# Layer-norm rows from VectorE to ScalarE, attention's value products two steps at a time, and ScalarE's pair copies between its two exponentials

## What is computed

```
def _layernorm(x, axis=-1, eps=1e-05):
    m = jnp.mean(x, axis=axis, keepdims=True)
    v = jnp.var(x, axis=axis, keepdims=True)
    return (x - m) / jnp.sqrt(v + eps)
...
    h = _layernorm(x, axis=-1) * (1 + ca) + sa
    x = x + ga * _L0_attn_ref(h, ...)      # q, k l2-normed; softmax(q k^T / 8) v; Wo; bo
    h = _layernorm(x, axis=-1) * (1 + cb) + sb
    x = x + gb * _L0_ffn_ref(h, ...)       # router, top 2 of 8 experts, capacity, shared expert
```

## Time and profile before

| | |
|---|---|
| three runs | 1409.37, 1414.08, 1416.97 us (median 1414.08) |
| the profiled execution: its own time, its span | 1406.78 us, 1405.0 us |
| mean granted TensorE clock | 0.959 |
| busy: PE, PEld | 1262.1 us (90%), 828.6 us (59%) |
| busy: DVE, ACT, POOL | 1107.3 us (79%), 952.9 us (68%), 858.0 us (61%) |
| idle of TensorE before line L585 until VectorE's L810 | 33.2 us, 14 times |

### The profile page before, as it was taken

The page is one execution under the profiler, slowest core; times in us unless marked ns, Lnnn a source line. Parts: engine busy times, 40 slices in busy tenths (PEclk is TensorE's granted clock), DMA queues, the critical chain, the costliest instruction groups (busy, mean ns, idle before and its releaser), DMA issues. The chain is left out here.

```text
span 1405.0 us, 31811 instructions
## 1 busy us (share of the span) xinstructions
PE 1262.1 (90%) x9674; PEld 828.6 (59%) x9674; DVE 1107.3 (79%) x1995; ACT 952.9 (68%) x2014; POOL 858.0 (61%) x1659
## 2 busy tenths in 40 slices
PE   4899999989999999999899999999994477899997
PEld 4555565656555565556566555666552355677775
DVE  3778878878878887788788788877873996788887
ACT  3677677767666776677677766777762565777776
POOL 2577666766666776666667667676754664444443
PEclk8899999999999999999999999999998699999999
DMA  5000000000000000000000000000002000535341
GB/s 131 2 2 1 2 1 2 2 4 2 1 4 2 2 2 4 2 2 2 4 1 2 3 2 2 2 1 2 2 1 75 1 0 9 131 86 104 89 89 38
DMA packets 53202, 28.60 MB, mean 20 GB/s; under 512 B 8720, under 2 KB 51224, under 8 KB 53016
## 3 DMA queue, kind: packets, MB, share of 16 engines
q1 hardware_dynamic: 51832, 25.99, 7.7%
q10 hardware_dynamic: 1184, 0.40, 0.1%
HBM read 24.16 MB, written 2.23 MB: 19 GB/s over the span
## 5 line engine op out<-in xcount | busy, mean ns | idle before, releaser
L697 ACT ACTIVATE probs<-bank,neg_max 128x512 f32<-128x512 f32 x512 | 347.5, 684 | 280.3 <-DVE neg_max L815 259.5
L815 DVE TENSOR_REDUCE neg_max<-bank 128x1 f32<-128x512 f32 x512 | 329.3, 685 | 165.4 <-PE bank L516 162.0
L556 PE MATMUL bank<-probsT,qkv 128*64 128x512 f32 x1024 | 280.7, 628 | 0.9 <-DVE oT L832 0.9
L516 PE MATMUL bank<-operands 64*128 64x512 f32 x1536 | 255.9, 439 | 0.9 <-DVE operands L810 0.5
L993 POOL TENSOR_TENSOR inv_wide<-inv_sum,consts 128x512 f32<-128x512 f32 x64 | 66.5, 1039 | 237.7 <-DVE inv_sum L826 237.7
L532 PEld LDWEIGHTS T<-ident,probs 64*128 64x128 f32 x4096 | 173.6, 142 | 40.3 <-issue 10.2
L532 PE MATMUL T<-ident,probs 64*128 64x64 f32 x4096 | 173.6, 226 | 1.5 <-issue 0.7
L486 PEld LDWEIGHTS bank<-operands,hT_h 128*128 128x128 f32 x254 | 48.2, 190 | 213.0 <-issue 209.4
L516 PEld LDWEIGHTS bank<-operands 64*128 64x128 f32 x1536 | 128.4, 190 | 63.5 <-issue 44.2
L1627 POOL TENSOR_TENSOR hid_l<-gated,hid_h 128x512 fp32r<-128x512 f32 x64 | 89.4, 1397 | 123.3 <-ACT hid_h L1544 123.3
L977 POOL TENSOR_TENSOR sq<-qkv 128x256 f32<-128x256 f32 x252 | 150.9, 615 | 11.9 <-ACT qkv L676 9.7
(11 more groups left out here) (235 smaller groups left out, 2399.7 us busy)
## 6 DMA issues: line engine op xcount, KB each, us to landing
probsT<-gate_scratch SPq DMA_DIRECT2D x64, 256.0 KB, 4.9
out<-x_all SPq DMA_DIRECT2D x8, 256.0 KB, 2.3
probsT<-in_L_ffn_fc_w SPq DMA_DIRECT2D x1, 1024.0 KB, 9.4
raw<-in_L_attn_Wq SPq DMA_DIRECT2D x1, 512.0 KB, 4.4
raw<-in_L_attn_Wk SPq DMA_DIRECT2D x1, 512.0 KB, 7.3
raw<-in_L_attn_Wv SPq DMA_DIRECT2D x1, 512.0 KB, 8.6
raw_o<-in_L_attn_Wo SPq DMA_DIRECT2D x1, 512.0 KB, 8.7
probsT<-in_L_ffn_sh_w SPq DMA_DIRECT2D x2, 256.0 KB, 2.7
```

The lines of the kernel that those rows point to most:

```text
L516: last = nc.tensor.matmul(s_bank(hp, 2 * pair + head)[:], own[rows, q, toks], own[rows, k], start=((q, k) == (QH, KH)), stop=(q == QL))
L556: last = nc.tensor.matmul(O_BANK[rows, :], qkv[:, hp % 4, j, cols], probsT[:, hp % 2, head, j], start=(j == 0), stop=(j == NT - 1), skip_g ...
L697: nc.scalar.activation(probs[:, i % 4], s_bank(hp, i)[:], ACT.Exp, bias=neg_max[:, i:i + 1], accum_out=row_sum[:, hp % 2, i:i + 1]).then_i ...
L815: nc.vector.reduce_max(neg_max[:, i:i + 1], s_bank(hp, i)[:], AX.X, negate=True).then_inc(max_done, 1)
```

## The change

Three edits. First, the rows of the layer norm: VectorE additionally writes the negative mean (4 numbers a row of partitions), GpSimd multiplies it by the inverse deviation (`ln_shift`) after its Newton iteration, and ScalarE computes x * rstd + shift in four instructions of 128x128 in place of VectorE's four. ScalarE does this in the same pair, after its copy of k and ahead of its exponentials; in the opening stage it does so after its sixth weight copy, and after the last slot ahead of `modulate2`. Second, TensorE does steps 2 and 3 of the value products together in pair 0, and steps 0 and 1 together in pair 2; pairs 1 and 3 have none. Third, ScalarE's copy of T2 in pairs 1 and 3 stands between the two exponentials of the pair instead of behind both.

```
             def aggregate(dve, count):
...
                 nc.vector.tensor_scalar(var_eps[:], mean_var[:, :, 1], LN_EPS, None, ALU.add).then_inc(ve_done, 1)
+                nc.vector.tensor_scalar(neg_mean[:], mean_var[:, :, 0], -1.0, None, ALU.mult).then_inc(nm_done, 1)
...
-            def ln_rows(dve, b, count):
-                dve.wait_ge(ln_step, NEWTON_OPS * (count + 1))
-                after(dve, hlnT_ready, count)
+                pool.wait_ge(nm_done, count + 1)
+                pool.wait_ge(ln_step, NEWTON_OPS * (count + 1))
+                nc.gpsimd.tensor_tensor(ln_shift[:], neg_mean[:], rstd[:], ALU.mult).then_inc(shift_done, 1)
+
+            def ln_rows(act, b, count):
+                act.wait_ge(shift_done, count + 1)
+                after(act, hlnT_ready, count)
                 for t in range(NT):
-                    last = nc.vector.tensor_scalar(h_ln[:, t], tile_of(b, t), mean_var[:, t, 0:1], rstd[:, t:t + 1],
-                                                   ALU.subtract, ALU.mult)
+                    last = nc.scalar.activation(h_ln[:, t], tile_of(b, t), ACT.Identity, scale=rstd[:, t:t + 1],
+                                                bias=ln_shift[:, t:t + 1])
                 last.then_inc(hln_done, 1)
...
-                            if pair < 2 and earlier >= 2:
-                                weigh_values(u - 2, hp - 2, pair + 2)
-                            if pair >= 2 and earlier >= 1:
-                                weigh_values(u - 1, hp - 1, pair - 2)
+                            if pair == 0 and earlier >= 2:
+                                weigh_values(u - 2, hp - 2, 2)
+                                weigh_values(u - 2, hp - 2, 3)
+                            if pair == 2 and earlier >= 1:
+                                weigh_values(u - 1, hp - 1, 0)
+                                weigh_values(u - 1, hp - 1, 1)
...
+                            if main and pair == 3 and norm_of(b, hp):
+                                ln_rows(act, *norm_of(b, hp))
                             if main:
                                 exponentials(u, hp, 2 * pair)
-                                exponentials(u, hp, 2 * pair + 1)
                             if pair == 1 and earlier >= 1:
                                 copy_transposed(u - 1, hp - 1, 3)
                             if pair == 3 and main:
                                 copy_transposed(u, hp, 1)
+                            if main:
+                                exponentials(u, hp, 2 * pair + 1)
...
-                            if rows and pair == 3:
-                                ln_rows(dve, *rows)
```

More of the change, by code:

```diff
@@ L155, in adaln_attention_moe @@
             rstd_t = sb("rstd_t", [P, NT])
+            neg_mean = sb("neg_mean", [P, NT])
+            ln_shift = sb("ln_shift", [P, NT])
             st1_done = sem("st1_done")
@@ L161, in adaln_attention_moe @@
             hln_done = sem("hln_done")
+            nm_done = sem("nm_done")
+            shift_done = sem("shift_done")
             hlnT_ready = sem("hlnT_ready")
@@ L297, in _ @@
                                                  ACT.Copy).then_inc(s_wh, 1)
+                            if j == 5:
+                                act.wait_ge(x0_in, 16)
+                                ln_rows(act, 0, 0)
                     @block.vector
@@ L317, in _ @@
                                                     ALU.subtract).then_inc(s_wl, 1)
-                            if j == 5:
-                                ln_rows(dve, 0, 0)
                         dve.wait_ge(s_small, 9 * 16)
@@ L461, in adaln_attention_moe, with norm_of @@
             t_pair = T2[:].rearrange("p a (k q) -> p a k q", q=DH)
+            def norm_of(b, hp):
+                if hp == YT_HP and not is_const(b, 0):
+                    return b - 1, h2_nth(b - 1)
+                if hp == H1T_HP - 1 and not is_const(b, LAST):
+                    return b + 1, h1_nth(b + 1)
+                return None
             with nc.Block() as block:
@@ L662, in _ @@
                     slot(B, 0, main=False)
-                    for j in (2, 3):
-                        weigh_values(HP * B - 1, HP - 1, j)
+                    weigh_values(HP * B - 1, HP - 1, 2)
+                    weigh_values(HP * B - 1, HP - 1, 3)
                     project_out(LAST, 3, (r_copied, HP * B), (y_more, 3 * LAST + 2))
@@ L781, in _ @@
                         high_h2(q)
+                    act.wait_ge(x1_done, B)
+                    ln_rows(act, LAST, h2_nth(LAST))
                     modulate2(LAST)
@@ L881, in first_part @@
                             take_mod(mod2, (GA, GA_BO, CB, SB), b, mod2_done, (h2_done, b))
-                    def norm_of(b, hp):
-                        if hp == YT_HP and not is_const(b, 0):
-                            return b - 1, h2_nth(b - 1)
-                        if hp == H1T_HP - 1 and not is_const(b, LAST):
-                            return b + 1, h1_nth(b + 1)
-                        return None
                     def norm_first(b, hp, pair):
@@ L965, in _ @@
                     guess_std(dve, nth)
-                    ln_rows(dve, LAST, nth)
                     logits(LAST)
```

## The result

The change makes the kernel **slower: 1450.55 us** median of four runs (1443.88 to 1457.74) against 1415.38 of before beside it (1409.37 to 1416.97). The ratio is 1.0257, 95% interval 1.0195 to 1.0319, so it is slower without doubt, and by 2% or more most likely. The forecast was 1431, with 1408 to 1450: the direction was right, the amount some 20 us short, and the median lies 0.5 us outside the range.

What follows compares the result with a forecast made beforehand. TensorE was taken to bound most slots, with VectorE's `low_k` in pair 3 and GpSimd's chain just behind. The terms summed to +17.5 us, so against 1414.1 us the forecast was 1431, range 1408 to 1450.

Steps and rivals of the forecast that it cites:

- 30 ordinary slots: Slots without norm event or loop end: merged products +0.71 us, wait for ScalarE's copy +0.16, so 30 x 0.87 = +26.1.
- twelve norm events of batches 1 to 6: Layer-norm slots 0 and 3, each with the slot behind: six at -0.6 us, six at -0.5, together -6.6.
- norm event of batch 7: The layer-norm event of batch 7: +0.5 us, with less to win because its clock did not fall.
- five ends of the loop body: At the branch TensorE arrives 1.00 us earlier and pair 3 keeps its gain: -0.12 us each, -0.6 together.
- last two slots, slot 0 of batch 0: The last two slots were put at +1.5 us and slot 0 of batch 0 at -1.4.
- opening and tail: Opening stage loses about 0.4 us, the norm after the last slot gains about 2.4: -2.0 together.
- Rival 2: Pair 3 keeps its shortening: 59 slots 1.0 us shorter, 1372 us; chance 0.10.
- rival 5: No effect of the merge, a second product step costs 1.00 us too: 1449 us; chance 0.04 with the rest.
- The four tiles: ScalarE's layer-norm instructions of an event: 0.8 to 3.2 us, taken as 2, costing nothing because GpSimd is later.
- rival 1: GpSimd does not bind the norm slots; an event gives -2.1 us instead of -0.55: 1413 us; chance 0.15.
- -0.5 us for the two slots together: Slots 3 and 4: transposes of q come 1.4 us earlier, the doubled product in pair 2 adds 0.86.
- rival 3: New stalls of about 2 us at L495 bring 1.2 GHz stretches: +13 to +20 us, 1444 to 1451; chance 0.14.

Runs made afterwards that it cites:

- after_again: The changed kernel once more, unaltered, on the same chip as `after_fill`: 1452.27 us, 1.030 of before.
- sq_back: `after_poolsq` with value products merged only in pair 2; steps 2 and 3 stand apart in pairs 0 and 1: 1411.90 us, 1.001 of before.
- after_poolsq: The changed kernel with GpSimd's squares ahead of its split of the attention output in slots 0 and 3: 1419.36 us, 1.005 of before.
- after_fill: The changed kernel plus seven matmuls with unread results ahead of pair 2's projection in slots 1 and 4, batches 1 to 6: 1436.56 us, 1.019 of before.
- sq_front: `after_poolsq` with value products merged only in pair 0; steps 0 and 1 stand apart in pairs 2 and 3: 1381.07 us, 0.979 of before.
- ln_only: The kernel before with the first edit alone, the layer-norm rows on ScalarE: 1390.69 us, 0.985 of before.

## Why the prediction was wrong, and what in it held

The profiled executions differ by +46.8 us, the sum was +17.5 (and 1414.1 + 17.5 is 1431.6, which I put down as 1431). By its own terms:

| term | forecast | measured |
|---|---|---|
| 30 ordinary slots | +26.1 | +32.2 |
| twelve norm events of batches 1 to 6 | -6.6 | +9.9 |
| norm event of batch 7 | +0.5 | +0.5 |
| five ends of the loop body | -0.6 | +3.0 |
| last two slots, slot 0 of batch 0 | +0.1 | +2.7 |
| opening and tail | -2.0 | -1.4 |

In the profile of `after_again`, 5 us shorter, the ordinary slots measure +28.9, the norm events +6.6 and the loop ends +4.0: these terms move by 1 to 3 us from one execution to the next.

**Right.** The ordinary slot: 23 of the 30 (all but slot 5 of batches 1 to 7) measure +0.82 on average against +0.87, with each step where it was put: second product 0.87, pair 1 at its floor of 2.55, the 0.16 us for ScalarE's copy (0.67 more without the third edit), and pair 3 held at S3 + 3.04. `sq_back` shows that last floor is what costs: the merge in pair 2 takes 41 us, the one in pair 0 ten. Rival 2, by which pair 3 would have kept its shortening, is thus refuted, and so is rival 5. The four tiles take 1.64 us, inside my 0.8 to 3.2 and below the 2 that I took; the page "ScalarE: Activation LUTs" of the Trainium skill (what ACT_TABLE_LOAD costs) had given an estimate of 1.6, and the trace agrees. The stall of the norm slots moved and did not go, with GpSimd as its cause; `ln_poolsq` and `after_poolsq` refute rival 1. The tail gave -2.3 for -2.4.

**Wrong: "-0.5 us for the two slots together".** For the norm events I let the old stall take its half clock with it and took none for the new one, though I named that case as rival 3. Where the new stall is followed by the full clock, the term nearly holds: in batch 4 slots 3 and 4 take 15.40 + 18.02 = 33.42 us against 33.47. What is missing to my -0.5 is GpSimd's chain: inversion to inversion 17.62 us, where I had worked out 17.15, because VectorE begins its sum 0.48 behind the end of the squares (504.11 to 504.59) in the event of slot 3. But in five of six batches slot 4 is 1.5 us longer than that, and in three of six slot 1 is 1.5 longer: 5 x 1.46 + 3 x 1.50 = 11.8 us at half clock behind the new stall, which carries most of the norm events' miss of 16.5. `after_fill` tests it without touching any wait of GpSimd: with the stall filled, half clock is gone from slots 1 and 4 in every batch, and 15.7 us of the 21 by which `after_again` (1452.3) exceeds my 1431 go away.

**Wrong as well: +0.87 for slot 5.** I gave the idle time that the merge puts ahead of `between` no price in clock. In slot 5, where the router's narrow matmuls follow it, five of six batches run 1.55 us longer: 7.8 us of what "ordinary slots" lists, and without it they would stand at +24.4. No rival of mine named this place.

With the first of the two, rival 3 came true: I had priced it at 13 to 20 us more, 1444 to 1451. Its price for one event, 1.0 to 1.5, was right, but only 8 of the 12 looped events paid it, 11.8 us, and 1431 + 12 would be 1443; that the time still lies in its band is in part luck, since slot 5, the loop ends and the last slots, which it doesn't name, made up the rest. Its chance of 0.14 was the mistake. My evidence was the wait of 1.89 us at the branch with the full clock behind it, against 2.49 us with half clock in the earlier trace rows. The new stall is 1.81 us, shorter than the one at the branch, and brings half clock in five of six batches in slot 4: the length of a stall alone doesn't tell, so the earlier trace rows was no evidence for another place in the cycle. With a case on either side the rival deserved about even chances, and the range an upper end beyond 1451. The page "TensorE: Matmul & The Clock Gate" of the Trainium skill (the HAM clock gate) says that activity is what releases the clock from its slow default. The experiments agree in slots 1 and 4, where seven matmuls in place of the wait kept the full clock. That idle time added to every slot would cost clock, as I read the rule, they bear out for slot 5 alone; in slots 2, 3 and 6 the same idle time cost none.

**Wrong, and smaller: the loop ends.** TensorE reaches the branch 1.00 us earlier, as I said, but then idles 2.14 to 2.91 us instead of 1.89, with half clock behind one of them: +3.0 instead of -0.6.

**Size and spread.** The four runs of the changed kernel fall in line with their clock: from 109.6 us at half clock in the whole span (1443.9 us) to 145.6 (1457.7), some 0.38 us for each, as expected of `after_again`, whose runs give 0.46. Before ran in a band of 7.6 us, the changed kernel in one of 13.9.

**Open.** Why the idle time at the branch grew; why VectorE's start behind the squares takes 0.48 us in one of the two norm slots and 0.13 in the other; where the 0.17 us ahead of L519 in `sq_front` come from; and why the half clock comes in some batches and not in others where the rows ahead of it read alike (batch 4 against 3). That the merge costs some 60 us on `ln_only`, 49 on `ln_poolsq` and 47 on before fits the clock, but was only argued from the half-clock times, not tried.

**A better kernel.** `ln_poolsq`, the first edit with GpSimd's squares first and without the other two, takes 1370.3 us, 3.0% below before and some 80 us below the change.

## What to carry to other kernels

Work moved between parts of a fixed cycle is worth only what the next floor lets through: measure each part's slack from a place where TensorE has too little to do, before you shift a whole product out of it. When a stall is taken away, find the engine that ends next and look at the order of its own queue; here an exchange in GpSimd's order was worth 20 us, and the 48 us of busy time taken off VectorE 23. And price every new stall of TensorE twice, as idle time and as the half-clock stretch that may follow it; a short one counts too where narrow matmuls stand behind it. When two such stretches follow each other, look for a kernel that has one without the other before you give them one cause.

## What the runs showed of the hardware

- A stall of TensorE of 1.7 to 1.8 us in an otherwise dense stream was followed by a stretch of some 3.4 us at half clock (1.2 GHz) in 15 of 24 cases (the changed kernel twice, slots 1 and 4), and each cost 1.5 us. With the same stall filled with matmuls it came in none of 12.
- An idle time of 0.84 us was followed by such a stretch where eight matmuls of 8 columns, 0.96 us to the next start, stood behind it (29 of 42 cases, slot 5 in seven profiles), and in none of the slots 2, 3 and 6 of batches 1 to 6, where other work did.
- VectorE's four tiles of normed rows took 3.39 us beside GpSimd's operations, but 1.11 in the opening stage of before, where GpSimd was idle:

```profile
14.32 1.11 DVE L200 TENSOR_SCALAR h_ln<-x_all,mean_var,rstd 128x128 f32<-128x128 f32 x4
```

  So two thirds of what the first edit takes off VectorE was waiting, not work. The norm after the last slot shows it tile by tile (a row of GpSimd's timeline, then the view of line L200 from 1079 to 1084 us: least, median and greatest duration in ns):

```profile
1079.33 3.70 POOL L137 TENSOR_TENSOR operands<-h_all,operands 128x512 fp32r<-128x512 f32 x3
```

```profile
L200 DVE TENSOR_SCALAR h_ln<-x_all,mean_var,rstd x4: 335/1277/1297, 1079.4 to 1083.0; 128x128 f32<-128x128 f32 x4
```

  Three tiles beside GpSimd's three operations of 1.26 us each took 1.26 to 1.30, and the fourth, which starts as GpSimd is done, took 0.34. GpSimd itself lost nothing: its three squares take 1.75 us in the earlier trace rows and 1.76 after, and the two operations ahead of them 1.04 and 1.27 beside VectorE's tiles, 1.04 and 1.28 without. ScalarE's tiles take 1.64 us beside the same GpSimd rows. The section "Who interferes with whom" of "SBUF — State Buffer" in the Trainium skill describes a port pair shared by VectorE and GpSimd that one of them locks for a whole instruction; these times agree with it.
